# Gating the recurrent states straight out of PSUM: one VectorE product in place of a ScalarE copy and a GpSimd product

## The reference

```
xi, z = split(einsum('btd,ed->bte', x, Win), 2)
lam   = exp(-8 * softplus(omega) * sigmoid(xi @ Wl.T + bl))
v     = xi @ Wv.T + bv
for t in 1..191:                                  # the state h has 512 channels for each sequence
    vh, vv = sum(v_t * h), sum(v_t * v_t)
    Qh = h - 2 * v_t * (vh / vv)
    h  = lam_t * Qh + (1 - lam_t) * x_t
out = einsum('bti,di->btd', silu(z) * h, Wout)    # the product silu(z) * h is what the change moves
```

## Time and profile before

| | us |
|---|---|
| median of 3 runs | 1030.51 |
| lowest and highest run | 1027.21, 1032.54 |
| the profiled execution's own time | 1034.37 |
| its span in the trace | 1032.6 |
| PE busy | 934.5 |
| DVE busy | 786.5 |
| ACT busy | 592.1 |
| POOL busy | 545.4 |

### The profile page before, as it was taken

The page is one execution under the profiler, slowest core; times in us unless marked ns, Lnnn a source line. Parts: engine busy times, 40 slices in busy tenths (PEclk is TensorE's granted clock), DMA queues, the critical chain, the costliest instruction groups (busy, mean ns, idle before and its releaser), DMA issues. The chain is left out here.

```text
span 1032.6 us, 19334 instructions
## 1 busy us (share of the span) xinstructions
PE 934.5 (91%) x5800; PEld 837.2 (81%) x5800; DVE 786.5 (76%) x2393; ACT 592.1 (57%) x1174; POOL 545.4 (53%) x652
## 2 busy tenths in 40 slices
PE   2689999999999999869799999999999999963998
PEld 2689999999999999765587888887888888852887
DVE  3678777777777777652588898988999999972676
ACT  1346666666666666634566676666666666621442
POOL 4156676767676765445244454545555554422573
PEclk9889999999999999988989999999999999975999
DMA  5001111111111140012999999999999999982310
GB/s 208 21 26 42 42 42 41 41 41 41 41 41 41 44 171 22 17 27 76 102 128 142 149 159 139 157 141 152 151 156 150 146 163 141 135 96 94 123 62 21
DMA packets 134814, 96.32 MB, mean 93 GB/s; under 512 B 11208, under 2 KB 129104, under 8 KB 134096
## 3 DMA queue, kind: packets, MB, share of 16 engines
q1 hardware_dynamic: 133200, 91.20, 58.3%
q0 software_dynamic: 1536, 4.20, 1.4%
HBM read 31.92 MB, written 13.11 MB: 44 GB/s over the span
## 5 line engine op out<-in xcount | busy, mean ns | idle before, releaser
L315 POOL TENSOR_TENSOR gelu_lo<-gelu_out,gelu_hi 128x384 fp32r<-128x384 f32 x128 | 151.0, 1208 | 29.9 <-DVE gelu_hi L529 29.4
L944 POOL TENSOR_TENSOR B_decayed_u<-B_scan_in 128x512 f32<-128x512 f32 x48 | 62.0, 1292 | 97.1 <-DMA B_scan_in<-B_stage 88.5
L708 PE MATMUL psA<-ternary_down,gelu_hi 128*128 128x256 f32 x384 | 96.9, 291 | 6.9 <-POOL gelu_lo L315 6.3
L652 PE MATMUL psA<-x2T_hi,ternary_up 128*128 128x384 f32 x256 | 94.7, 370 | 3.4 <-DVE residual L642 3.2
L708 PE MATMUL psA<-ternary_down,gelu_lo 128*128 128x256 f32 x384 | 93.3, 282 | 0.0
L652 PE MATMUL psA<-x2T_lo,ternary_up 128*128 128x384 f32 x256 | 88.5, 346 | 0.0
L932 POOL TENSOR_TENSOR B_y<-B_scan_in,B_states 128x512 f32<-128x512 f32 x48 | 61.9, 1289 | 41.9 <-ACT B_states L1003 41.9
L1192 PEld LDWEIGHTS psB<-B_partial_dots,B_minus_same_batch 128*128 128x128 f32 x384 | 66.4, 194 | 21.8 <-DVE B_partial_dots L1076 10.6
L1180 PE MATMUL psB<-Win_hi,B_x_hi 128*128 128x512 f32 x192 | 83.6, 435 | 0.0
L708 PEld LDWEIGHTS psA<-ternary_down,gelu_hi 128*128 128x128 f32 x384 | 72.2, 188 | 11.4 <-POOL gelu_lo L315 10.2
L1092 DVE SCALAR_TENSOR_TENSOR psB<-B_decayed_u,psB 128x128 f32<-128x128 f32 x192 | 68.0, 354 | 12.7 <-PE psB L1192 12.2
(11 more groups left out here) (251 smaller groups left out, 3329.5 us busy)
## 6 DMA issues: line engine op xcount, KB each, us to landing
B_scan_in<-B_stage SPq DMA_DIRECT2D x192, 256.0 KB, 8.1
patches<-in_patches SPq DMA_DIRECT2D x16, 384.0 KB
B_residual<-layer_out SPq DMA_DIRECT2D x48, 128.0 KB, 5.2
out_dram<-B_residual SPq DMA_DIRECT2D x48, 128.0 KB, 5.0
C_raw<-in_experts SPq DMA_DIRECT2D x8, 768.0 KB, 4.4
layer_out<-residual SPq DMA_DIRECT2D x32, 128.0 KB, 1.8
layer_out<-residual SPq DMA_DIRECT2D x32, 64.0 KB, 2.0
raw_Wl<-in_upT SPq DMA_DIRECT2D x1, 1024.0 KB, 9.1
```

The costliest lines, as they stand in the source:

```text
L315: nc.gpsimd.tensor_tensor(act_l[:, k, :], act[:, k % DEEP, :], act_h[:, k, :].bitcast(F32), ALU.subtract).then_inc(s["ffn_lo"], 1)
L652: last = nc.tensor.matmul(out, a, b, start=(n == 0), stop=(n == len(terms) - 1))
L708: last = nc.tensor.matmul(ps[:, 6 + k // 2, (k % 2) * D:(k % 2 + 1) * D], x[:, c, k * P:(k + 1) * P], dn_w[:, c, :], start=(c == 0 and x i ...
L944: nc.gpsimd.tensor_tensor(lu[:, j % 2], ring[:, j % R_RING, :, LAM, :], ring[:, j % R_RING, :, U, :], ALU.mult).then_inc(s["lu"], 1)
```

## The change

In part_b, VectorE multiplies GATE in the ring by the states in their PSUM bank and writes B_y; this stands at the top of iteration i, ahead of step(i,0), and is for tile i-1. ScalarE's copy, GpSimd's product, the buffer B_states and the semaphore hs are gone. The wait ahead of reusing a state bank is now on y instead of hs. PE and SP wait for y as before, and the new instruction waits for the transposes of the tile that used its B_y slot two tiles ago (yT), as GpSimd's did.

```diff
-        hs = sb("B_states", [P, 2, 4, P])
...
                 tanh_z gate lu scan dot hs y yT y_hi y_lo wout res""".split():      # hs is taken out of this list
...
         def _(pool):
             for i in range(FIRST, LAST):
-                if has(i - 1):
-                    j = i - 1
-                    pool.wait_ge(s["hs"], j + 1)
-                    wait(pool, s["yT"], j - 1)
-                    nc.gpsimd.tensor_tensor(y[:, j % 2], ring[:, j % R_RING, :, GATE, :], hs[:, j % 2],
-                                            ALU.mult).then_inc(s["y"], 1)
...
         def _(sc):
-                if has(i - 1):
-                    j = i - 1
-                    sc.wait_ge(s["scan"], decayed(4 * j + 4) if j + 1 < TT else stepped(4 * j + 3))
-                    wait(sc, s["y"], j - 1)
-                    nc.scalar.activation(hs[:, j % 2].rearrange("p a b -> p (a b)"), ps[:, STATE + j % 2, :],
-                                         ACT.Copy).then_inc(s["hs"], 1)
...
             def ahead(t):
                 if k == 0:
                     wait_arrived(v, j)
-                    wait(v, s["hs"], j - 1)
+                    wait(v, s["y"], j - 1)
...
             for i in range(FIRST, LAST):
                 if i == 0:
                     ahead(0)
+                if has(i - 1):
+                    j = i - 1
+                    v.wait_ge(s["scan"], stepped(4 * j + 3))
+                    wait(v, s["yT"], j - 1)
+                    nc.vector.tensor_tensor(y[:, j % 2], ps[:, STATE + j % 2, :].rearrange("p (r c) -> p r c", r=4),
+                                            ring[:, j % R_RING, :, GATE, :], ALU.mult).then_inc(s["y"], 1)
                 step(i, 0)
```

More of the change, by code:

```diff
@@ L850, in part_b @@
                 stats aggr ve rstd shift applied xT x_hi x_lo l v xi z tanh_l log_decay lam vsq rs u drive
-                tanh_z gate lu scan dot hs y yT y_hi y_lo wout res""".split():
+                tanh_z gate lu scan dot y yT y_hi y_lo wout res""".split():
             s[name] = ctx.enter_context(nc.semaphore("B_" + name))
```

## The result

The changed kernel takes 1046.58 us (median of 4 runs, 1041.68 to 1049.09) where the kernel before takes 1029.40 (4 runs, 1027.21 to 1032.54): a ratio of 1.016, 95% interval 1.011 to 1.021. Two later measurements of the same file gave 1.014 (1.009 to 1.019) and 1.0115 (1.0065 to 1.016). It is slower, as forecast: every interval lies above 1, though the size is under 2%. The first median lies 7 us above the forecast of 1039.5. That is 1.6 us above the upper end of 1045 that the forecast gave itself, and 0.4 us inside the 8-in-10 range. The first difference between medians is 17.2 us, the later two are 12.4 and 11.3 us.

A forecast was written before the change was run, and what follows sets the result against it. TensorE bounds quiet iterations, then VectorE; late ones run at the DMAs' pace. Loop +7.7 and start +0.1 make +7.8 us; carried to the median, 1038.3 to 1040.9, forecast 1039.5 us (own range 1034.3 to 1045; 8-in-10 range 1032.5 to 1047).

The forecast's parts named there:

- Bound: Loop: 28 quiet iterations bound by TensorE at 8.53 us, VectorE 0.35 behind; 15 late ones wait for DMA arrivals.
- What goes, at 0: ScalarE's copy (0.60 us) and GpSimd's product (1.30) set no pace in the loop, so removing both counts 0.
- What comes, 0.60 with 0.25 covered: VectorE's product before step(i,0) costs 0.60 us, 0.25 covered by the wait for a dot; quiet iterations 8.53 to 8.88.
- Start and end, 0.1 and 0: At the loop's start VectorE's wait for PE covers the product, about +0.1 us; the earlier last y gains 0.
- they stay at 137.1, +0: The loop's 15 late iterations, at the DMAs' pace of 9.14 us on average, absorb the product: 137.1 us, +0.
- From the loop to the median: Whole kernel: +7.8 us on the profiled 1034.4, carried to the median, gave 1038.3 or 1040.9; forecast put between.
- The signs it named: Loop: product 0.68 us, next start 0.60; quiet iterations 8.88, no dot wait, PE idle 0.35; B_scan_in waits under 8.4.
- three signs of being wrong: In the loop, quiet iterations stay at 8.55, late ones grow by 0.6 each, or PE still has no idle time.
- DMAs as the only bound: Rival, chance 0.12: a loop tile costs about 8.79 us whatever VectorE does; +0 to +3, about 1032.
- Latency loop with the full +16.8: Rival, chance 0.09: gate, DMA, arrival, next gate form a loop; late iterations pay 0.60, more become late; 1047.
- The faster case: Rival, chance 0.04: SP's DMAs come out earlier, arrivals stop being late, product under 0.25 us on VectorE; 1019.
- The dear product: Rival, chance 0.05: VectorE's product, for its runs of 128, costs up to twice 0.60 us; about 1060.

## Why the prediction was right, and where its size was off

**Bound.** Quiet iterations in the kernel before are at 8.55 with and without late arrivals around them (halved DMAs), so the reading of two kinds of iteration held. That TensorE alone bounds them is too strong: with the log decay moved elsewhere TensorE did the same matmuls in 8.27 to 8.39 us in ten iterations. It may be that the dots, for which each of the two engines waits on the other, tie them to a common pace of 8.53; no run tests this.

**What goes, at 0.** Shown: the product added with nothing removed gives a loop (388.49) and a ratio (1.015) like those of the changed kernel.

**What comes, 0.60 with 0.25 covered.** Shown from both sides. A quarter product (0.30) costs nothing; a quiet iteration takes 8.86 to 8.87, forecast 8.88; a second product with no slack left costs 0.57. The neighbour L1134 was the right row for an instruction that the trace didn't have. Each of the two products starts its successor 0.60 after itself, not 0.68. The main rule in "The DRAIN you can't avoid" (the Trainium skill, VectorE: DVE Perf Modes) would have made the second one 0.68, and the loop shows 0.57. The forecast put the price of that rule at 3.4 us, which is 0.08 in all 43 iterations; with its own 28 it would be 2.2.

**Start and end, 0.1 and 0.** The start of the 5th gate stayed (530.62 before, 530.58 after), and PE's last transposes were held by the output product as forecast.

**The late iterations, "they stay at 137.1, +0".** This is the term that was mis-sized. The forecast took them to be at the pace of the DMAs, so that they keep their 9.14 us and absorb the product. What they do is something else: fewer are late (15 and 11 in the two profiles of the kernel before, 7, 6 and 6 in the three of the changed one), but one that is still late pays all of 0.60 on top of its remaining wait (10.35 = 8.18 + 1.17 + 0.40 + 0.60). By the profile's rows 36 x 8.86 + 7 x (8.18 + 3.8 / 7 + 0.40 + 0.60) = 319.0 + 68.1 = 387.1, near the measured 388.6. Most of the rest is that ScalarE also waited for arrivals that were early enough for VectorE: in six more iterations L1148 starts 0.06 to 0.27 us late behind it.

The landing times in the traces show where the absorption comes from, and why it is small. The last of a tile's four DMAs lands 13.2 to 13.5 us (median) after the start of the tile's gate in all profiles of the two kernels, and 13.7 with two products: how fast VectorE goes makes no clear difference. VectorE asks for the tile in its next iteration, 8.55 + 5.46 = 14.0 us after the gate in the kernel before and 8.86 + 5.46 = 14.3 in the changed one. So the product's 0.60 is paid behind the arrival, and only 0.32 comes off the wait ahead of it: about 0.3 us is left to pay where a tile was late by more than that, and next to nothing where it was late by less. With the waits of the first profile, 10 above 0.32 us and 5 below, that makes an estimate of 28 x 0.32 + 10 x 0.28 + 5 x 0.07 = 12.1 us, near the +10.6 of the two first profiles and well above the forecast's 7.7.

The loop's excess over 43 quiet iterations (367.5 before, 381.1 after, from the halved DMAs) was 10.5 and 8.4 us in the two profiles before, and 7.4, 5.8 and 3.9 in the three after. So some 9.5 - 5.7 = 3.8 us of the 13.6 were absorbed, where the forecast had 15.05 (43 x 0.35) - 7.7 = 7.4. The forecast's loop, +7.7, should have been 13.6 - 3.8 = +9.8; the measured loops give 386.8 - 377.0 = +9.8 in the mean.

**From the loop to the median.** The forecast also took the profiled execution of before as if it stood for the median. It had more late arrivals (15) than the second one (11). Between medians the change costs 11 to 17 us where the loop has 9.8, and 16.3 with halved DMAs, where the loop has 13.6. What is left, 1.5 to 7.4 us with whole DMAs and 2.7 with halved ones, is open. All three profiles of the changed kernel fell on executions at or near the lowest of their group (1041.68, 1040.64 and 1038.88 us), so the slower ones were not seen. The stretch behind the last instruction of part_b, part_c in the main and the same code in all, took 93.4 to 99.8 us and adds its own scatter: 95.7 in both profiles of the kernel before, 93.5 in all three of the changed one, 95.7 and 98.9 in the two with halved DMAs.

**The signs it named.** Quiet iterations of 8.88, no wait for the dot, 0.68 and 0.60 for the product, and less waiting for B_scan_in all came out. TensorE's idle time did not: 0.11 us in the quiet iteration of the profile, not 0.35 (last section). Of its three signs of being wrong, quiet iterations at 8.55 didn't come. "Late ones grow by 0.6 each" came in part: a late one holds the whole 0.60, but 0.32 of it comes off its wait. "PE still has no idle time" came nearly to the letter; it was a poor sign, since TensorE's busy time stretched.

**Rivals.** DMAs as the only bound: out, by the halved DMAs. Latency loop with the full +16.8: the total came out near it in the first measurement (17.2 between medians), but not its mechanism, since late arrivals fell and an earlier issue brought nothing. Its one true part is that a late iteration holds the whole product. The faster case: out; it needed a product that costs VectorE under 0.25 us, and with the quarter product, which is nearly that, the kernel took as long as before and not 1019. The Trainium skill's rule (GPSIMD Engine Reference, section "4.1 Engine selection") had the ratio of the two engines about right, 0.69 against 1.30 us in the rows, and says nothing on which one has time to spare. The dear product: out at 0.69 us. Its price of about 1060 was also too low for a product of twice 0.60: the kernel with two products took 1069.89 us.

## What to carry to other kernels

Before moving work to a faster engine, find the slack on the engine that takes it at the very place where it goes (from start to start, against the spacing of back-to-back instructions), and the idle time on the engine that gives it up. Here 0.25 us was there for 0.60, and 1.9 us was taken from engines that were waiting anyway. When iterations are sometimes late for a transfer, ask on which side of the wait the new work stands, and by how much it moves the moment of asking. Only that much is absorbed; the rest is paid, late or not. And look at who else stands behind the late transfer: a third staging slot was the only edit with the output left right whose ratio lies clear of 1 on the fast side.

## What the runs showed of the hardware

TensorE's busy time did not show its slack. In the quiet iteration of the changed kernel, where VectorE no longer waits for a dot, TensorE is busy 8.75 of 8.86 us, hardly less than the 8.53 of 8.53 of the earlier trace rows:

```profile
804.68:813.54 8.86, 8.75 (x52) 7.30 (x51) 8.41 (x30) 5.35 (x12) 3.04 (x6) 1.00 1.22 157
```

Over the loop with halved DMAs the same 2146 matmuls are busy 366.63 us in one kernel and 375.06 in the other at the same clock. A sign that could be trusted was on the other side: VectorE's wait for a dot, 27 times before and once after.

TensorE's weight loads (PEld) did not stretch in this way: 315.63 and 313.16.

The time from a tile's gate to the landing of its last DMA (median of 43 tiles) was 13.2 to 13.9 us in every kernel with whole DMAs, at 8.55 us an iteration as at 9.46, issued 0.77 us after the gate's start or 1.53, and 8.8 with half the bytes.

The DMA share stayed at 1.16 to 1.21 in all kernels with whole DMAs, with 5 late arrivals or 18, and was 0.60 and 0.61 with half the bytes. It did not tell whether transfers were late.
